# Products of 512 columns become two groups of 256 columns in the same bank

## The chip, the cores and the metric

The kernel runs on one core of a Trainium2 chip. The metric is device time in microseconds for one execution; lower is better. TensorE multiplies a stationary operand of 128 x 128, which a weight load brings in first, with a moving operand of up to 512 columns, and adds the result into one bank of PSUM (128 partitions, 512 float32 columns a bank). ScalarE (ACT) and VectorE (DVE) read PSUM, GpSimd (POOL) and SyncE (SP) start transfers.

## The reference

One block of a network on x of 4 x 2048 x 256 (float32):

```python
h = _layernorm(x, axis=-1) * (1 + ca) + sa
x = x + ga * _L0_attn_ref(h, ...)      # a gated linear recurrence over the 2048 steps
h = _layernorm(x, axis=-1) * (1 + cb) + sb
x = x + gb * _L0_ffn_ref(h, ...)       # 8 experts, each takes its best 512 rows of each of 4 batches
```

The recurrence: `u = h @ W_in`, two gates `sigmoid(u @ W_gx)` and `sigmoid(u @ W_ga)`, a scan over the steps, and `@ W_out`. The experts: softmax of scores over 8 experts, the 512 best rows of each expert and batch, `gelu(rows @ w1) @ w2` with a hidden width of 1024, weighted and added back into the rows.

## The kernel before, in words

It has two stages, written out engine by engine, with semaphores between the engines; the order on each engine is the order in the text.

The recurrence handles the 8192 rows in 16 groups of 512 (GT). In each of its steps TensorE transposes a group (line 1768), multiplies an earlier one by W_out (line 1852), forms two gates and u (`channels`, line 1749), and scores an older one (line 1874). `channels` computes two blocks (m) of 128 output channels; each block is one bank of PSUM and one call of `product`.

The experts are 32 units (8 experts x 4 batches), of 512 rows (CAPK) each. In unit u TensorE first transposes the gathered rows (line 1899), then does the second layer of the unit before (`layer2`, line 1925: 4 tiles of 128 rows, 24 matmuls of 256 columns each), then the first layer of its own (`layer1`, line 1953: 8 blocks m of 128 hidden channels, 6 matmuls of 512 columns each). Behind the first two blocks of most first layers stands `make_list` (line 428), 16 matmuls of 8 columns in bf16, for the unit after next. In the units at the start single bf16 matmuls (line 293) count hits for the choice of rows; they wait for VectorE.

Products are done in float32r with each operand split into a high and a low part: `PASSES` has the three pairs that are multiplied, so a product over 256 inputs (KD = 2 blocks) is 6 matmuls into one bank, the first with `start`, the last with `stop`. Behind the last one a semaphore tells ScalarE that the bank is full (`f_H` in the first layer); ScalarE takes the gelu (line 1210) and rounds it to the high part (line 1214), VectorE forms the low part (line 1540). Four banks are used in turn for the first layer (`h_bank`), and TensorE waits on `f_hf` before it fills one again.

Of the kernel before, what the change touches and what calls it, by code (L numbers as in the profile page):

```python
# [14 lines left out]
P = 128  # L15
# [33 lines left out]
def adaln_kernel(nc, x, W_in, b_in, W_gx, b_gx, W_ga, b_ga, a_param, W_out, b_out, gate_w, w1, w2, c, wmod, out):  # L49
# [5 lines left out]
    GT = 512  # L55
# [4 lines left out]
    CAPK = CAP * S // E  # L60
# [20 lines left out]
    with keep:  # L81
# [341 lines left out]
        def make_list(pe, u):  # L423

            for t in range(ST):
                if t % (ST // 2) == 0:
                    pe.wait_ge(f_pl, 2 * u + t // (ST // 2) + 1)
                ins = pe.matmul(list_psum(u), place[u % 2][:, t, :], vals_u[u % 2][:, t, :, :],  # L428
                                start=(t == 0), stop=(t == ST - 1))
            ins.then_inc(f_lm, 1)  # L430
# [33 lines left out]
        def sbr(name, shape, dt=F32):  # L464
            return recur.enter_context(nc.sbuf_tensor(name, shape, dt))
# [54 lines left out]
        hT_z = [sbr(f"hT_z{q}", [P, KD, GT], F32R) for q in range(2)]  # L520
# [89 lines left out]
        def rounds_in(s):  # L610

            n = [(s - PAIR_AT) * ROUNDS_IN - 2 + j for j in range(ROUNDS_IN)]
            return [v if 0 <= v < BITS else None for v in n]
# [10 lines left out]
        def sbf(name, shape, dt=F32):  # L624
            return moe.enter_context(nc.sbuf_tensor(name, shape, dt))

        w1_s = [[sbf(f"w1_0{q}", [P, KD, H], F32R) for q in range(2)]]
# [3 lines left out]
        xT = [sbf(f"xT{q}", [P, KD, CAPK], F32R) for q in range(2)]  # L631
# [86 lines left out]
        def h_bank(u, m):  # L718

            return H_bank[m % 4 if u else m % 2]  # L720
# [19 lines left out]
        def rounds_of(u):  # L740

            if u >= CHOSEN_IN:
                return [None] * 6
            here = [rounds_until(u) + j for j in range(PER_UNIT[u])]
            return here + [None] * (6 - len(here))
# [3 lines left out]
        with nc.Block() as block:  # L749
# [994 lines left out]
            def _(pe):  # L1744
                def product(out_, stationary, moving, first, last):

                    terms = [(k, q) for k in range(KD) for q in PASSES]
                    for j, (k, (qs, qm)) in enumerate(terms):
                        ins = pe.matmul(out_, stationary(qs, k), moving(qm, k), start=(first and j == 0),  # L1749
                                        stop=(last and j == len(terms) - 1))  # L1750
                    return ins

                def channels(out_, w, n=None, then=None):

                    for m in range(KD):
                        ins = product(out_[:, m, :], lambda q, k: w[q][:, k, m * P:(m + 1) * P], lambda q, k: hT_z[q][:, k, :],
                                      True, True)
                        if m == 0:
                            count(n)
                        if m == 0 and then is not None:  # L1760
                            then(pe, 0)
                    return ins
# [101 lines left out]
                def score(g):  # L1864

                    pe.wait_ge(r_x1T, g + 1)
                    pe.wait_ge(r_lo, min(g + 4, NG))
                    if g == 0:
                        pe.wait_ge(s_gw, 2)
                    if g >= 1:  # L1870
                        pe.wait_ge(r_sr, g)
                    for t in range(TT):
                        for k in range(KD):
                            ins = pe.matmul(S_tok[:, t, :], x1T[:, k, t * P:(t + 1) * P], Gb[:, g // GB, k, :],  # L1874
                                            start=(k == 0), stop=(k == KD - 1))
                    ins.then_inc(r_S, 1)

                def count(n):

                    if n is not None:  # L1880
                        sum_hits(pe, 0, n)
# [21 lines left out]
                def count_later(u, n):  # L1903

                    if n is not None:
                        pe.wait_ge(f_xf, u + 1)
                        sum_hits(pe, 1, n)
# [25 lines left out]
                def layer1(u):  # L1933

                    n = UNITS[u][0]
                    v = u + LISTED if u + LISTED < NU else None
                    late = u == CHOSEN_IN
                    pe.wait_ge(f_x, u + 1)
                    pe.wait_ge(f_ws, 4 * n + 2)
                    for m in range(KH):  # L1940
                        if u == 0 and m == 1:
                            score(NG - 1)
                        if v and m == (5 if u == 0 or late else 2):
                            make_list(pe, v)
                        if u == 0 and m >= 2:
                            pe.wait_ge(f_hf, m - 1)
                        elif u == 1 and m < 2:
                            pe.wait_ge(f_hf, KH + m - 1)
                        elif u >= 1:
                            pe.wait_ge(f_hf, KH * u + m + 1 - 4)  # L1950
                        terms = [(k, q) for k in range(KD) for q in PASSES]
                        for x_, (k, (qs, qm)) in enumerate(terms):
                            ins = pe.matmul(h_bank(u, m), w1_s[n % 2][qs][:, k, m * P:(m + 1) * P], xT[qm][:, k, :],  # L1953
                                            start=(x_ == 0), stop=(x_ == len(terms) - 1))
                        ins.then_inc(f_H, 1)
                        if u == 1 and m % 2 == 0:
                            count_later(u, rounds_of(u)[2 + m // 2])
                        if u != 1 and m in (1, 3, 5):
                            count_later(u, rounds_of(u)[3 + m // 2])
# [21 lines left out]
                for s in range(1, NG + 1):  # L1981
                    _, c_, _, d, e_ = stages(s)
                    n = rounds_in(s)
# [23 lines left out]
                    else:  # L2007
                        pe.wait_ge(r_p, c_)
                    channels(psA, Wa, n[0], sum_ties if s == NG else None).then_inc(r_A, 1)
                    if e_ is not None:  # L2010
                        pe.wait_ge(r_x1T, e_ + 1)
                    if c_ >= 1:
                        pe.wait_ge(r_tx, c_)
                    channels(psX, Wx, n[1], turn_probs if s == PAIR_AT else None).then_inc(r_X, 1)
                    if e_ is not None:
                        score(e_)
                    if s == NG:
                        sum_selected(pe, 0)
                    count(n[2])
                    pe.wait_ge(r_ta, c_ + 1)  # L2020
                    channels(psA, Wu, n[3], turn_slots if s == NG else None).then_inc(r_U, 1)
                    if s == 1:
                        mod_columns("ln2", 3)
# [15 lines left out]
                for u in range(NU):  # L2039
                    if u >= 1:  # L2040
                        turn(u)
                        layer2(u - 1, between_tiles(u))
                    layer1(u)
# [26 lines left out]
```

## Time and profile before

| | us |
|---|---|
| median of 3 runs | 1106.22 (1104.28 to 1106.46) |
| the profiled execution | 1105.63 |
| its span, first to last instruction | 1103.8 |
| TensorE busy in it | 1057.6 |
| mean granted clock of TensorE, as a share of full | 0.979 |

The span is cut into busy times of engines, a chain of waits followed back from the last instruction, and groups of instructions by line. A mean duration of a matmul is longer than its share of TensorE's time, since matmuls overlap; the spacing of a run of matmuls is its time divided by their number. In the chain a piece such as "PE psum L1925 x96" is a run of matmuls of one line in which nothing else was waited for.

### The profile page before, as it was taken

The page shows a single profiled execution, that of the slowest core. Times are in us where ns is not written, and L with a number is a line of the kernel's source. Part 1 is how long each engine was busy: PE and PEld are TensorE (multiplying, and loading weights), DVE is VectorE, ACT ScalarE, POOL GpSimd, SP SyncE. Part 2 cuts the span into 40 slices and gives each one's busy share as a digit, 9 for nine tenths or more (in the row PEclk, how much of TensorE's full clock was granted, in tenths as well). Part 3 has the DMA queues.
Part 4 walks back from the last instruction along what each step waited for, and adds up shares of the span by engine and source line. Part 5 has one row for each costly group of instructions (what it writes and reads, how often), then busy time and mean ns, then how long its engine had stood idle before and what let it go on. Part 6 is the DMA issues. An engine that isn't in the chain of part 4 may idle for free.

```text
span 1103.8 us, 18701 instructions
## 1 busy us (share of the span) xinstructions
PE 1057.6 (96%) x6922; PEld 932.2 (84%) x6922; DVE 726.5 (66%) x1680; ACT 781.1 (71%) x1237; POOL 461.2 (42%) x422
## 2 busy tenths in 40 slices
PE   7899999999798999999999999999999999999985
PEld 6778888888686888888999888999888999888875
DVE  5678999998767888965456455455455454477354
ACT  4658888887566777787666777775777766786741
POOL 2123432331343445444445444445544544454533
PEclk8999999999889999999999999999999999999988
DMA  7056756623348545555223545235343442379650
GB/s 253 10 124 191 232 146 141 154 59 57 78 124 102 149 116 121 157 123 125 55 40 80 123 87 138 53 81 136 80 111 80 92 102 39 69 216 309 160 186 39
DMA packets 96891, 130.85 MB, mean 119 GB/s; under 512 B 17312, under 2 KB 82464, under 8 KB 95776
## 3 DMA queue, kind: packets, MB, share of 16 engines
q1 hardware_dynamic: 62960, 84.11, 24.0%
q0 software_dynamic: 33024, 44.75, 23.2%
q8 instruction: 55, 0.90, 0.3%
q10 hardware_dynamic: 816, 0.79, 0.2%
q14 instruction: 36, 0.29, 0.1%
HBM read 78.96 MB, written 42.27 MB: 110 GB/s over the span
## 4 chain that ended last, share of the span: by engine, by line
PE 79%; DVE 7%; ACT 6%; issue 4%; DMA 2%; POOL 1%; SPq 1%; DVEq 0%; ACTq 0%; POOLq 0%
PE psum L1953 30%; PE psum L1925 30%; PE psum L1749 7%; PE psum L1852 4%; PE psum L1899 2%; PE psum L1768 2%; PE psum L1874 2%; DVE st L1237 1%; PE psum L428 1%; DMA w_raw<-ffn_rows 1%; DVE hs L1301 1%; DMA out_x<-res_t 1%; DVE x L1313 1%; ACT tx L1078 1%; ACT hT_z L1028 1%
## 5 line engine op out<-in xcount | busy, mean ns | idle before, releaser
L1925 PE MATMUL psum<-w,hidT 128*128 128x256 f32 x3072 | 374.1, 282 | 5.9 <-issue 4.5
L1953 PE MATMUL psum<-xT,w 128*128 128x512 f32 x1536 | 373.9, 399 | 4.9 <-DVE xT L1527 3.6
L1925 PEld LDWEIGHTS psum<-w,hidT 128*128 128x128 f32 x3072 | 364.9, 189 | 8.4 <-issue 6.4
L1953 PEld LDWEIGHTS psum<-xT,w 128*128 128x128 f32 x1536 | 286.5, 190 | 65.1 <-DVE xT L1527 3.8
L1540 DVE TENSOR_TENSOR hidT<-hf,hidT 128x512 fp32r<-128x512 f32 x256 | 176.5, 692 | 248.6 <-ACT hidT L1214 237.5
L960 POOL DMA_INDIRECT ffn_rows<-rows_y,idx_cur x120 | 210.7, 1755 | 229.4 <-issue 179.2
L450 POOL DMA_INDIRECT rows_in<-x_rows,idx_cur x128 | 139.4, 1089 | 177.5 <-DVE idx_cur L421 147.9
L1210 ACT ACTIVATE hf<-psum 128x512 f32<-128x512 f32 x256 | 151.2, 591 | 26.8 <-PE psum L1953 15.5
L1214 ACT ACTIVATE hidT<-hf 128x512 fp32r<-128x512 f32 x256 | 161.8, 632 | 8.1
L1116 ACT ACTIVATE rows_y<-psum,g_cur 128x256 f32<-128x256 f32 x124 | 51.9, 470 | 163.1 <-PE psum L1925 155.4
L410 DVE TENSOR_TENSOR place<-row_id,slot_u 128x1024 bf16<-128x1024 bf16 x64 | 76.3, 1222 | 1.1
L1484 DVE TENSOR_TENSOR w<-w_raw,w 128x1024 fp32r<-128x1024 f32 x60 | 71.4, 1220 | 0.3 <-issue 0.2
L1527 DVE TENSOR_TENSOR xT<-xf,xT 128x1024 fp32r<-128x1024 f32 x32 | 39.2, 1225 | 48.3 <-ACT xT L1106 46.6
L1145 ACT ACTIVATE w<-w_raw 128x1024 fp32r<-128x1024 f32 x60 | 60.1, 1046 | 12.3 <-DMA w_raw<-in_L_ffn_w 12.3
L1152 ACT ACTIVATE rows_in<-rows_in 128x256 f32<-128x256 f32 x128 | 66.3, 595 | 2.7 <-DMA rows_in<-x_rows,idx_cur 2.7
L1852 PE MATMUL psum<-Wout,hs 128*128 128x256 f32 x256 | 61.9, 398 | 2.4 <-ACT gb_bc L1091 2.4
L911 POOL TENSOR_SCALAR ve<-x 128x4 f32<-128x4 f32 x16 | 3.5, 222 | 139.6 <-DVE x L1241 139.5
L1055 ACT ACTIVATE ta<-psum,half_ba 128x512 f32<-128x512 f32 x32 | 20.3, 685 | 53.6 <-PE psum L1749 53.6
L1852 PEld LDWEIGHTS psum<-Wout,hs 128*128 128x128 f32 x256 | 50.2, 201 | 9.5 <-issue 2.6
L1749 PE MATMUL psum<-hT_z,Wa 128*128 128x512 f32 x192 | 52.4, 421 | 3.3 <-DVE p_t L1278 1.8
L1749 PE MATMUL psum<-hT_z,Wu 128*128 128x512 f32 x192 | 50.2, 405 | 0.0
L1100 ACT ACTIVATE xf<-psum,sbc,cb 128x512 f32<-128x512 f32 x64 | 45.9, 766 | 5.5 <-PE psum L1899 5.5
(206 smaller groups left out, 1225.3 us busy)
## 6 DMA issues: line engine op xcount, KB each, us to landing
w_raw<-in_L_ffn_w SPq DMA_DIRECT2D x30, 1024.0 KB, 11.3
x_rows<-x SPq DMA_DIRECT2D x16, 516.0 KB, 4.0
x_buf<-in_L_attn_x SPq DMA_DIRECT2D x16, 512.0 KB, 5.8
ffn_rows<-scratch SPq DMA_DIRECT2D x8, 1024.0 KB, 8.5
x_buf<-bias_bc POOLq DMA_DIRECT2D x16, 512.0 KB, 7.7
scratch<-x_rows SPq DMA_DIRECT2D x12, 512.0 KB, 8.6
out_x<-scratch SPq DMA_DIRECT2D x12, 512.0 KB, 7.9
w_raw<-ffn_rows SPq DMA_DIRECT2D x12, 512.0 KB
```

What stands on the lines that cost most here:

```text
L410: dve.tensor_tensor(place[n][:, at, :], row_id[:].unsqueeze(1).to_broadcast([P, ST // 2, P]), slot_u[n][:, at, :].to_broadcast([P, ST // 2 ...
L450: pool.indirect_dma_start(rows_in[u % 2][:, t, :], None, xr_dram[b], bass.IndirectOffsetOnAxis(ap=idx_cur[u % 4][:, t:t + 1], axis=0))\
L960: pool.indirect_dma_start(acc_dram[b], bass.IndirectOffsetOnAxis(ap=idx_cur[u % 4][:, t:t + 1], axis=0), rows_y[u % 2][:, t, :], None, com ...
L1152: ins = act.activation(x_u[:, t, 0:D], x_u[:, t, 0:D], ACT.Identity, bias=x_u[:, t, D:D + 1], scale=x_u[:, t, D + 1:D + 2])
L1210: act.activation(hf[m % HF][:], h_bank(u, m), ACT.Gelu_apprx_tanh).then_inc(f_hf, 1)
L1214: act.activation(hidT[0][:, m, :], hf[m % HF][:], ACT.Copy).then_inc(f_hh, 1)
L1484: dve.tensor_tensor(parts[1][:, at, :], raw[:, at, :], parts[0][:, at, :].bitcast(F32), ALU.subtract).then_inc(f_ws, 1)
L1540: dve.tensor_tensor(hidT[1][:, m, :], hf[m % HF][:], hidT[0][:, m, :].bitcast(F32), ALU.subtract).then_inc(f_hl, 1)
L1749: ins = pe.matmul(out_, stationary(qs, k), moving(qm, k), start=(first and j == 0), stop=(last and j == len(terms) - 1))
L1852: ins = pe.matmul(O_tok[:, t, :], hs[d % 2][:, k, t * P:(t + 1) * P], Wout[d // GB % 2][:, k, :], start=(k == 0), stop=(k == KD - 1))
L1925: ins = pe.matmul(y_tile(u, t), hidT[qs][:, k, t * P:(t + 1) * P], w2_s[n % 2][qm][:, k, :], start=(x_ == 0), stop=(x_ == len(terms) - 1))
L1953: ins = pe.matmul(h_bank(u, m), w1_s[n % 2][qs][:, k, m * P:(m + 1) * P], xT[qm][:, k, :], start=(x_ == 0), stop=(x_ == len(terms) - 1))
```

## The change

`channels` and `layer1` do each product in two halves of 256 columns: six matmuls for columns 0 to 255 of the bank, then six for columns 256 to 511. Each half has its own `start` and `stop`. The semaphore behind a first-layer product hangs on the last matmul of the second half, as the last of the product; in `channels` the count of hits comes behind both halves. The weights, the moving operand, the banks and the readers are as before.

```diff
                     for m in range(KD):
-                        ins = product(out_[:, m, :], lambda q, k: w[q][:, k, m * P:(m + 1) * P], lambda q, k: hT_z[q][:, k, :],
-                                      True, True)
+                        for half in (slice(0, GT // 2), slice(GT // 2, GT)):
+                            ins = product(out_[:, m, half], lambda q, k: w[q][:, k, m * P:(m + 1) * P],
+                                          lambda q, k: hT_z[q][:, k, half], True, True)
                         if m == 0:
                             count(n)
...
                         terms = [(k, q) for k in range(KD) for q in PASSES]
-                        for x_, (k, (qs, qm)) in enumerate(terms):
-                            ins = pe.matmul(h_bank(u, m), w1_s[n % 2][qs][:, k, m * P:(m + 1) * P], xT[qm][:, k, :],
-                                            start=(x_ == 0), stop=(x_ == len(terms) - 1))
+                        for half in (slice(0, CAPK // 2), slice(CAPK // 2, CAPK)):
+                            for x_, (k, (qs, qm)) in enumerate(terms):
+                                ins = pe.matmul(h_bank(u, m)[:, half], w1_s[n % 2][qs][:, k, m * P:(m + 1) * P], xT[qm][:, k, half],
+                                                start=(x_ == 0), stop=(x_ == len(terms) - 1))
                         ins.then_inc(f_H, 1)
```

## Rows read from the trace of the kernel before

**Rows 1.** The page's first part: busy us, share of the span, instructions.
```profile
PE 1057.6 (96%) x6922; PEld 932.2 (84%) x6922; DVE 726.5 (66%) x1680; ACT 781.1 (71%) x1237; POOL 461.2 (42%) x422
```
**Rows 2.** Busy time by stretch: two of the recurrence, then one unit.
```profile
core 0: us, PE busy (x) PEld busy (x) DVE busy (x) ACT busy (x) POOL busy (x), PEclk, DMA share, GB/s
93.00:108.40 15.40, 15.40 (x86) 13.34 (x85) 12.96 (x33) 12.33 (x18) 5.48 (x9) 1.00 0.56 155
187.50:203.60 16.10, 15.99 (x90) 13.20 (x89) 14.70 (x48) 13.55 (x21) 5.14 (x9) 1.00 0.44 127
643.20:666.94 23.74, 23.74 (x171) 21.49 (x170) 12.23 (x20) 17.33 (x30) 11.26 (x9) 1.00 0.40 90
```
**Rows 3.** Groups by line: count | busy us, mean ns of one | idle before.
```profile
L1925 PE MATMUL psum<-w,hidT 128*128 128x256 f32 x3072 | 374.1, 282 | 5.9 <-issue 4.5
L1953 PE MATMUL psum<-xT,w 128*128 128x512 f32 x1536 | 373.9, 399 | 4.9 <-DVE xT L1527 3.6
L1925 PEld LDWEIGHTS psum<-w,hidT 128*128 128x128 f32 x3072 | 364.9, 189 | 8.4 <-issue 6.4
L1540 DVE TENSOR_TENSOR hidT<-hf,hidT 128x512 fp32r<-128x512 f32 x256 | 176.5, 692 | 248.6 <-ACT hidT L1214 237.5
L1210 ACT ACTIVATE hf<-psum 128x512 f32<-128x512 f32 x256 | 151.2, 591 | 26.8 <-PE psum L1953 15.5
L1214 ACT ACTIVATE hidT<-hf 128x512 fp32r<-128x512 f32 x256 | 161.8, 632 | 8.1
```
**Rows 4.** The chain, 470 to 530 us: start us, us, what.
```profile
472.61 4.24 PE psum L1953 x18
...
477.73 10.89 PE psum L1925 x96
488.62 2.75 PE psum L1953 x12
491.37 0.40 PE psum L428 x16
491.77 8.36 PE psum L1953 x36
...
501.00 11.31 PE psum L1925 x96
512.31 2.80 PE psum L1953 x12
```
**Rows 5.** Groups by line, 483 to 487 and 506 to 510 us, TensorE.
```profile
L1925 PE MATMUL psum<-w,hidT 128*128 128x256 f32 x38 | 4.5, 276 | 0.0
...
L1925 PE MATMUL psum<-w,hidT 128*128 128x256 f32 x36 | 4.4, 281 | 0.0
```
**Rows 6.** The chain, 1016 to 1104 us.
```profile
1036.82 11.20 PE psum L1953 x48
...
1063.16 1.66 issue
```
**Rows 7.** The chain, 376 to 392 us.
```profile
378.27 0.88 PE psum L1899 x8
379.14 5.46 PE psum L1925 x48
384.60 0.02 PE psum L293
384.62 2.93 PE psum L1925 x24
```
**Rows 8.** The chain, 90 to 125 us.
```profile
93.47 5.57 PE psum L1749 x24
```
**Rows 9.** DMA queues: packets, MB, share of 16 engines.
```profile
q8 instruction: 55, 0.90, 0.3%
```
**Rows 10.** Waits over the span: us in total, times, longest.
```profile
PE psum L293 <- DVE hit L217: 5.5, 7, 1.1
```
**Rows 11.** Waits, 1040 to 1104 us.
```profile
PEld psum L1925 <- issue: 5.9, 9, 1.2
```

## The prediction

> **What bounds the kernel now.** I read the shares of busy time first: TensorE is busy 96% of the span and no other engine more than 71% [rows 1]. A share is a mean over stages, so I looked at single stages. In each stretch read of the first half (the recurrence) TensorE is busy without a gap or nearly so, and in the experts a whole unit of 23.74 us has 23.74 us of TensorE, at the full clock (1.00, 2.4 GHz), while ScalarE and VectorE have 6 and 11 us to spare [rows 2]. A microsecond added to the stream of products is therefore a microsecond of the kernel, and one taken away is a gain. The chain of waits agrees: its pieces in the experts are nothing but TensorE's lines [rows 4].
>
> So the question is one of spacing: how long from one product's start to the next. The groups by line say that 3,072 products of 256 columns (second layer) keep TensorE busy as long as 1,536 of 512 columns (first layer): 374.1 and 373.9 us [rows 3]. Column for column the two sizes cost the same; the mean durations (282 and 399 ns) overlap and must not be multiplied. These totals hide two different spacings, which the chain shows piece by piece [rows 4]:
> - 256 columns: 96 products in 10.89 us (113.4 ns each) in one unit and in 11.31 us (117.8 ns each) in the next, with nothing waited for in either. I call these the short and the long spacing. Mean durations change with them, 276 and 281 ns [rows 5].
> - 512 columns: 12 products that follow without a break take 2.75 us (229.2 ns) behind short ones and 2.80 us (233.3 ns) behind long ones. Where the list's 16 small products stand before them, they go back to the short spacing: pieces of 18 and 36 take 4.24 and 8.36 us, so 18 more cost 4.12 us, 228.9 ns each, with 0.12 us for the restart. A piece of 48 with no list in it stays long throughout (11.20 us, 233.3 ns) [rows 6].
>
> The spacing is thus a state that lasts until something breaks the stream, and that is newly chosen behind each break. I can't derive from the trace what chooses it.
>
> **The change, part by part.** It removes 1,536 + 576 products of 512 columns and adds twice as many of 256: 2,112 more products and as many more weight loads. Nothing else is issued: waits, signals, banks and readers stay, since the signal hangs on the last product of the second half and the count of hits stands behind both halves. No DMA and no queue is moved.
>
> *Weight loads.* They double in both places. The second layer already has a load for each 256 columns, and its loads (364.9 us busy) lie under 374.1 us of products [rows 3]; their cost is inside 113.4 or 117.8 ns, so I add nothing. If that cover failed, it would already show in the second layer.
>
> *First layer, 32 units of 8 products of 6.* Doubled, the short spacing gives 226.8 ns where one wide product takes 228.9, and the long one 235.6 where it takes 233.3. The sign hangs on the state. In a unit of the steady half, the first 12 become 24 that follow the second layer unbroken: 24 x 117.8 = 2.83 us against 2.80 if that is long (+0.03). The other 36 become 72 behind the list's break: 0.12 + 72 x 117.8 = 8.60 us if long (+0.24), 0.12 + 72 x 113.4 = 8.28 us if short (-0.08). I take long: the nearest row of 256 columns behind a small bf16 product is the pair of pieces behind the count of hits, 24 in 2.93 us, which less the same 0.12 us is 117 ns each; the piece before them, behind a transpose, is 48 in 5.46 us (113.8 ns) [rows 7]. Units before the steady half have most of their wide products short too, so 32 x 0.27 = 8.6 us; a product there sometimes waits for VectorE's count of hits (5.5 us over 7 waits [rows 10]), which hides a little, so +8.
>
> *Second layer.* Untouched, 0, if its state stays in each unit. What precedes it does change, and that is the largest unknown: a unit that goes from long to short gains 11.31 - 10.89 = 0.42 us, over some 24 units -10 us; the few short ones going long cost at most 2.
>
> *Recurrence, 576 products.* 24 take 5.57 us [rows 8], 232.1 ns each. Two narrow ones: 226.8 to 235.6, so from -3.1 to +2.0 us. Its breaks are again small products and counts, which stand nearest to [rows 7], so I take the long end; some of it hides in the stage's few waits: +1.
>
> *Evacuation.* A first-layer product of six takes 1.39 us (8.36 / 6); ScalarE's two passes over it take 0.591 + 0.632 = 1.22 us and VectorE's one 0.692 [rows 3]. Both stay under the new 1.36 to 1.41 us, so neither becomes the bound.
>
> *Supply of instructions.* 4,224 more instructions come through the queue that has 55 packets and 0.90 MB now [rows 9]; I take 0, since the second layer runs at that density for 11 us on end. Beside it stands the one stretch near the end where TensorE stops in small pieces with no releaser shown: pieces of "issue" up to 1.66 us [rows 6], and idle of 5.9 us in that window [rows 11]. If lack of instructions is its cause, it may grow or move: from -8 to +15 us.
>
> Sum: 8 + 0 + 1 = +9 us on the profiled execution's 1105.6 us (span 1103.8 and 1.8 around it): 1114.6. The median of the runs shown lies 0.6 us higher than that execution, well inside the other errors, so I leave the number.
>
> The rows show the extra as a state; the Trainium skill has a constant instead. Its page "TensorE: Matmul & The Clock Gate", section "Wait — 56ns, not 53.3ns?", puts a fixed cost of about 2.5 ns on every matmul at the full clock, whatever its columns. That speaks against splitting: 2,112 x 2.5 = 5.3 us, an estimate from that page, and 1110.9 us. The long rows agree with it (2 x 117.8 - 233.3 = 2.3 ns), the short ones (2 x 113.4 - 228.9 = -2.1 ns) do not.
>
> **The rivals.**
> - *The second layer's restart falls into the short spacing.* For: the pieces behind the transposes before the steady half are short: three of 48 in 5.46 us, of which one stands in [rows 7], and the 96 in 10.89 us of [rows 4]. Against: from 501 us on every steady unit is long. Per steady unit: second layer -0.42, the first 24 at 113.4 (2.72 against 2.80) -0.08, the other 72 long +0.24: -0.26; 24 units -6.2, the other eight +1.6, the recurrence +1 to -3: -4 to -8, 1098 to 1102 us. This ends on the other side. It decides as soon as more than about half of the steady units turn.
> - *The first layer goes short behind the list, the second stays long*, as wide products do there now. Per unit +0.03 - 0.08 = -0.05, over 32 units -1.6, recurrence +1 to -3: 1101 to 1105 us.
> - *Both go short.* 24 x -0.58 = -13.9, the rest -1 to -4: about 1089 us.
> - *Instructions run short* in the denser stream: the stretch near the end comes twice, or longer: +9 with 8 to 15 more, 1123 to 1130 us. Against it: no unnamed idle in the second layer elsewhere.
>
> **How the numbers follow.** Forecast (long behind the list, second layer as it is) 0.42; second layer turns short 0.26; only the first layer short 0.14; both short 0.11; instructions 0.07. The predicted time is the forecast's, 1114.6, with its own range 1109 to 1119 from the bounds of the recurrence and of the early units. For 8 in 10 I take in the second and third case and leave out the last two: 1096 to 1119. Faster by over 0.2% (2.2 us, about what a measurement of this kernel can tell from no change): 0.24 of the second case, 0.06 of the third, 0.11 of the fourth, 0.41. Within 0.2%: 0.02 and 0.08, 0.10. Slower: 0.42 and 0.07, 0.49.
>
> **What would show it.** In the profile after, the steady units' chain should have 24 products of line 1953's successor in about 2.83 us, 72 in 8.60 us, and 96 of the second layer still in 11.31 us; a unit of 24.0 us. Mean durations of 281 ns in both layers mean long, 276 short. If 72 take 8.28 us or the second layer 10.89 us, the state was misjudged, not the bound. Wrong altogether would be a unit in which TensorE has gaps, or a spacing of 256 columns outside 113 to 118 ns.

## The result, and the profile after

The changed kernel takes 1096.08 us (median of 4 runs, 1095.47 to 1098.32) where the kernel before takes 1106.34 beside it: a ratio of 0.9917, 95% interval [0.9904, 0.993]. It is 10 us faster where 8 us slower was forecast. The time lies outside the forecast's own range (1109 to 1119) and just inside the lower edge of the wider one (1096 to 1119), on the side that the forecast did not take.

The page of the profiled execution (span 1094.4 us; before 1103.8) begins with busy us, share and instructions of each engine, which answers to [rows 1]:

```profile
PE 1049.2 (96%) x9034; PEld 1030.4 (94%) x9034; DVE 726.0 (66%) x1680; ACT 779.2 (71%) x1237; POOL 462.4 (42%) x422
```

TensorE has 2,112 more products and still bounds. What it was given is seen only by stretch. This account is made from the starts of the same products in both traces:

| stretch | before to after, us |
|---|---|
| start to the first layer of unit 0 (recurrence) | -0.35 |
| to the first layer of unit 8 | +1.2 |
| units 8 to 27 | -5.6 |
| units 28 and 29 | +1.3 |
| first layer of unit 30 to the last second layer | -7.8 |
| last second layer and the end | +1.8 |

The chain after, 640 to 690 us (start us, us, what), answers to [rows 4]. L1926 is the second layer, L1955 the first, with the list left out, L1900 the transposes:

```profile
642.96 10.90 PE psum L1926 x96
653.86 2.72 PE psum L1955 x24
...
656.98 8.27 PE psum L1955 x72
665.25 0.87 PE psum L1900 x8
666.12 11.31 PE psum L1926 x96
677.43 2.83 PE psum L1955 x24
...
680.66 8.59 PE psum L1955 x72
```

The first unit is short in all three pieces (10.90, 2.72, 8.27), the second long in all three (11.31, 2.83, 8.59). The state lives through the list and is chosen anew behind the transposes. The units come as short, short, long, over and over: 23.16, 23.17 and 24.00 us, a mean of 23.44, where every steady unit before took 23.74.

The chain of the recurrence, to set beside [rows 8]:

```profile
93.33 5.70 PE psum L1749 x48
...
100.71 2.95 PE psum L1749 x24
```

The piece that took 5.57 us takes 5.70, so 118.8 ns a product: a third value, outside the 113 to 118 of the experts.

The chain after, near the end, to set beside the stops of [rows 6]:

```profile
1033.38 10.89 PE psum L1955 x96
...
1045.14 2.40 PE psum L1926 x21
1047.54 2.14 issue
1049.68 8.79 PE psum L1926 x75
1058.47 8.79 PE psum L1955 x72
```

The many small stops are gone. One of 2.14 us is left, at the 21st product, and the other 75 run through. The second layer of unit 30 takes 13.3 us from its first product to its last, before 19.2. Of the 7.8 us of this stretch it holds 5.9; the first layer of unit 31, after it, holds 1.4.

A part of both is TensorE's clock. The chain before has these two pieces behind the stops:

```profile
1065.55 2.71 PE psum L1925 x11
1068.26 12.30 PE psum L1953 x48
```

And by stretch (two of before, then the second layer of unit 30 after: us, TensorE busy and its products, granted clock, DMA share, GB/s):

```profile
1059.30:1064.10 4.80, 1.99 (x11) 1.00 0.62 209
1064.20:1070.90 6.70, 5.95 (x20) 0.50 0.46 177
1044.90:1058.30 13.40, 11.26 (x99) 1.00 0.48 180
```

Before, TensorE was idle for more than half of 4.8 us, and then the granted clock stood at 0.50 (1.2 GHz) from 1064.1 to 1071.0 us. There 11 products take 2.71 us where the long spacing gives 1.30, and the first layer of unit 31 takes 12.30 us where a piece of 48 takes 11.20 [rows 6]. So some 2.5 us of the 7.8 (1.4 + 1.1, an estimate from these pieces) are the lower clock behind the stops and not the stops themselves. The changed kernel runs this work at 1.00; it has a fall of 3.4 us earlier, from 1015.2 us, in the stretch of units 28 and 29 that came out 1.3 us longer.

### The profile page after: what moved, and what is told of

Same layout as the page of the kernel before. It is cut to its first block, busy times and chain, and to the rows that moved or that the text cites. A ratio compares the mean times of both kernels' runs of the same rounds, so it can differ in the third digit from the quotient of the medians.

```text
span 1094.4 us, 22925 instructions
## 1 busy us (share of the span) xinstructions
PE 1049.2 (96%) x9034; PEld 1030.4 (94%) x9034; DVE 726.0 (66%) x1680; ACT 779.2 (71%) x1237; POOL 462.4 (42%) x422
## 4 chain that ended last, share of the span: by engine, by line
PE 82%; DVE 5%; ACT 5%; issue 3%; DMA 2%; POOL 1%; SPq 0%; DVEq 0%; ACTq 0%; POOLq 0%
PE psum L1955 30%; PE psum L1926 29%; PE psum L1749 10%; PE psum L1853 4%; PE psum L1875 2%; PE psum L1900 2%; PE psum L1769 2%; PE psum L428 1%; DMA w_raw<-ffn_rows 1%; DVE st L1237 1%; ACT hf L1210 1%; PE psum L1803 1%; DMA out_x<-res_t 1%; ACT rows_in L1152 1%; DVE x L1313 0%
## 5 line engine op out<-in xcount | busy, mean ns | idle before, releaser
L1955 PE MATMUL psum<-xT,w 128*128 128x256 f32 x3072 | 374.5, 281 | 6.3 <-DVE xT L1527 3.6
L1955 PEld LDWEIGHTS psum<-xT,w 128*128 128x128 f32 x3072 | 363.8, 190 | 6.9 <-DVE xT L1527 3.8
L1926 PE MATMUL psum<-w,hidT 128*128 128x256 f32 x3072 | 365.4, 280 | 4.2 <-issue 2.1
L1926 PEld LDWEIGHTS psum<-w,hidT 128*128 128x128 f32 x3072 | 357.7, 188 | 5.1 <-DVE hidT L1540 2.8
L960 POOL DMA_INDIRECT ffn_rows<-rows_y,idx_cur x120 | 212.9, 1774 | 225.8 <-issue 177.4
L450 POOL DMA_INDIRECT rows_in<-x_rows,idx_cur x128 | 136.9, 1069 | 177.2 <-DVE idx_cur L421 147.5
L1853 PE MATMUL psum<-Wout,hs 128*128 128x256 f32 x256 | 59.5, 386 | 2.4 <-ACT gb_bc L1091 2.4
L1749 PE MATMUL psum<-hT_z,Wa 128*128 128x256 f32 x384 | 54.1, 298 | 4.2 <-DVE Wu L1340 2.0
L1749 PEld LDWEIGHTS psum<-hT_z,Wa 128*128 128x128 f32 x384 | 50.5, 197 | 5.7 <-DVE hT_z L1267 2.9
L1749 PE MATMUL psum<-hT_z,Wu 128*128 128x256 f32 x384 | 50.6, 286 | 0.0
```

The costliest lines, as they stand in the source:

```text
L450: pool.indirect_dma_start(rows_in[u % 2][:, t, :], None, xr_dram[b], bass.IndirectOffsetOnAxis(ap=idx_cur[u % 4][:, t:t + 1], axis=0))\
L960: pool.indirect_dma_start(acc_dram[b], bass.IndirectOffsetOnAxis(ap=idx_cur[u % 4][:, t:t + 1], axis=0), rows_y[u % 2][:, t, :], None, com ...
L1853: ins = pe.matmul(O_tok[:, t, :], hs[d % 2][:, k, t * P:(t + 1) * P], Wout[d // GB % 2][:, k, :], start=(k == 0), stop=(k == KD - 1))
L1926: ins = pe.matmul(y_tile(u, t), hidT[qs][:, k, t * P:(t + 1) * P], w2_s[n % 2][qm][:, k, :], start=(x_ == 0), stop=(x_ == len(terms) - 1))
L1955: ins = pe.matmul(h_bank(u, m)[:, half], w1_s[n % 2][qs][:, k, m * P:(m + 1) * P], xT[qm][:, k, half], start=(x_ == 0), stop=(x_ == len(te ...
```

## The experiments

Each run has its own measurement of the kernel before on the same chip. All ratios are to that, with the 95% interval. Patterns and times within a kernel come from the one profiled execution of each run; the mean unit runs from the second layer of unit 7 to that of unit 27. "Unit 30" is the time from the first to the last product of its second layer; "gathers" is how long behind that first product GpSimd starts the gathers of unit 31.

| run | ratio | steady second layers | mean unit, us | unit 30, us | gathers, us |
|---|---|---|---|---|---|
| before | 1 | all long | 23.74 | 19.2 | 5.3 |
| after | 0.9917 [0.9904, 0.993] | short, short, long | 23.46 | 13.3 | 10.4 |
| e14 (after again) | 0.9922 [0.9901, 0.9944] | short, short, long | 23.46 | 12.5 | 8.8 |
| e1 | 0.9894 [0.9878, 0.9909] | short, short, long | 23.46 | 12.7 | 8.8 |
| e2 | 0.9996 [0.9984, 1.0008] | all long | 23.74 | 18.2 | 5.3 |
| e3 | 0.9905 [0.9885, 0.9925] | all short | 23.50 | 12.9 | 9.5 |
| e4 | 1.0003 [0.9992, 1.0014] | all long | 23.77 | 18.5 | 5.3 |
| e5 | 0.9963 [0.9949, 0.9977] | short, short, long | 23.46 | 19.4 | 5.3 |
| e6 | 0.9942 [0.9926, 0.9959] | all long | 23.74 | 13.3 | 10.4 |
| e7 | 0.9913 [0.9897, 0.993] | all short | 23.53 | 12.8 | 9.9 |
| e8 | 0.9973 [0.9953, 0.9993] | long, short | 23.81 | 12.7 | 8.9 |
| e10 | 0.988 [0.986, 0.99] | all short | 23.25 | 12.9 | 9.4 |
| e11 | 0.9884 [0.9864, 0.9904] | all short | 23.27 | 13.2 | 10.1 |
| e12 | 0.9943 [0.9923, 0.9963] | long but the first | 23.72 | 12.7 | 9.5 |
| e15 | 0.9953 [0.9936, 0.9969] | short, short, long | 23.46 | 19.6 | 5.3 |
| e16 | 0.9999 [0.999, 1.0009] | all long | 23.74 | 21.6 | 5.3 |
| e17 | 0.992 [0.9903, 0.9936] | long but the first | 23.72 | 10.9 | 5.3 |
| e18 | 0.9939 [0.9921, 0.9957] | long but the first | 23.72 | 14.6 | 10.0 |
| e20 | 0.9978 [0.9961, 0.9995] | long but the first | 23.72 | 11.6 | 12.7 |
| e21 | 1.0008 [0.9995, 1.002] | all long | 23.74 | 19.3 | 5.3 |

### What chooses the state

Theory A: the state is chosen at each break of the stream, and hangs on the timing of that break, so a delay of some 25 ns changes the pattern. Theory B: the width of the products fixes it. (Theory C in the texts below, that the gain lies in the stops near the end, is taken up behind this part.)

**Each part of the change alone.** e1 leaves `channels` as before, e2 leaves `layer1` as before.

```diff
-                        for half in (slice(0, GT // 2), slice(GT // 2, GT)):
-                            ins = product(out_[:, m, half], lambda q, k: w[q][:, k, m * P:(m + 1) * P],
-                                          lambda q, k: hT_z[q][:, k, half], True, True)
+                        ins = product(out_[:, m, :], lambda q, k: w[q][:, k, m * P:(m + 1) * P], lambda q, k: hT_z[q][:, k, :],
+                                      True, True)
```

> Only the first layer's products are halved; gates and u stay 512 columns wide. Theory A (each break of the stream picks the short or the long spacing anew by its timing, and the width has no say in it): the recurrence gets back the 0.18 us per step that the halves cost there (two pieces of 5.57 and 2.90 us against 5.70 and 2.95), some 2 to 3 us over 16 steps, and the experts show some mixture of short and long units again, not necessarily the one of the changed kernel: 1089 to 1104 us. Theory B (narrow products in the first layer bring the second layer into the short spacing): two units in three short as in the changed kernel, 1093 to 1095 us. Theory C (the gain lies in the stretch near the end, where the kernel before stops 8 us with no releaser): 1100 us or less only if that stretch is free of stops here too.

```diff
-                        for half in (slice(0, CAPK // 2), slice(CAPK // 2, CAPK)):
-                            for x_, (k, (qs, qm)) in enumerate(terms):
-                                ins = pe.matmul(h_bank(u, m)[:, half], w1_s[n % 2][qs][:, k, m * P:(m + 1) * P], xT[qm][:, k, half],
-                                                start=(x_ == 0), stop=(x_ == len(terms) - 1))
+                        for x_, (k, (qs, qm)) in enumerate(terms):
+                            ins = pe.matmul(h_bank(u, m), w1_s[n % 2][qs][:, k, m * P:(m + 1) * P], xT[qm][:, k, :],
+                                            start=(x_ == 0), stop=(x_ == len(terms) - 1))
```

> Only gates and u are halved; the first layer stays 512 columns wide. Theory B: the experts are as in the kernel before, all steady units long in the second layer, 23.74 us each, and the recurrence costs 2 to 3 us more: 1108 to 1110 us. Theory A: the same recurrence, but the experts begin at another moment, so the steady units may go short in the second layer, 23.3 us each instead of 23.74: anything from 1097 to 1110 us. Theory C: if the stops near the end come from where TensorE stands in its stream of instructions, they may go away here, -6 to -8 us, with the units as before.

e1 has the whole gain, its pattern and the missing stops; e2 is at 0.9996, so halving gates and u alone changes nothing that can be measured. (The changed kernel's two ratios, 0.9917 and 0.9922, stand 2.5 to 3 us above that of e1; their intervals overlap with its own, and whether the gates' halves cost that much beside the others is open.) All that follows is in the first layer.

**A break 25 ns longer.** The list's first matmul is issued twice, in the changed kernel (e3) and in the one before (e4).

```diff
+                for _ in range(1 if t == 0 else 0):
+                    pe.matmul(list_psum(u), place[u % 2][:, t, :], vals_u[u % 2][:, t, :, :], start=True, stop=True)
                 ins = pe.matmul(list_psum(u), place[u % 2][:, t, :], vals_u[u % 2][:, t, :, :],
```

> The changed kernel with the first of the list's 16 small matmuls issued twice, so that each list's break lasts about 25 ns longer (32 lists, 0.8 us in all; the first of the two is overwritten). Theory A: the pattern of units (short, short, long) changes, all short (23.2 us each, 1091 us) or all long (24.0 us each, 1102 to 1106 us) or another mixture. Theory B: the pattern stays and the time is 1097 us.

> The kernel before with the same extra small matmul in each list, and no product halved. Theory A: the steady units, all long before, may turn short in the second layer (10.89 instead of 11.31 us), wholly or in part: 1096 to 1107 us, and then without any change of width. Theory B: all stay long, 1107 us. Theory C: the stops near the end change, since 64 instructions more lie before them: up to 8 us less with the units as before.

The chain of e3 (L1928 is the second layer, L1957 the first, L429 the extra matmul):

```profile
644.45 10.90 PE psum L1928 x96
655.34 2.72 PE psum L1957 x24
658.06 0.02 PE psum L429
...
658.49 8.59 PE psum L1957 x72
```

One small matmul more and the repeating three units are gone: every steady second layer is short, every piece of 72 long, so here the state changes at the list, which it did not do in the kernel without the extra matmul. That goes with theory A. The kernel with wide products does not move with the same edit, though: in e4 the second layers stay long, and the 36 products behind the list take 8.36 us as before. So what stands in the break matters, but the same addition does not act alike on both streams. An extra matmul adds an instruction and some 25 ns at once; no run tells the two apart.

**Two and three more**, with the gates wide (`range(2 ...)` and `range(3 ...)` in the same place, on e1).

> The first layer halved and gates wide, and each list's first small matmul issued three times, so each list's break is 50 ns longer (1.6 us over 32 lists). If the spacing behind a break is chosen by its timing, the pattern of units (short, short, long without the extra) changes: all short gives 23.2 us a unit and 15 us faster than before, all long 24.0 us and no gain. If the timing has no say, 9 to 10 us faster, with the same pattern.

> The same with the first small matmul issued four times, 75 ns longer a break (2.4 us in all). Chosen by timing: again another pattern, between 23.2 and 24.0 us a unit, from 14 us faster to no gain. Not chosen by timing: 8 to 9 us faster with the pattern short, short, long.

Two give the pattern of e3 (mean unit 23.53 us), three a new one: long, short, long, short (24.07 and 23.55 us). Breaks that differ by one small matmul a step thus gave three patterns, with the same products and the same columns. It is not the chance of one execution: the five traces with halves in the steady units and the breaks as they were (after, e14, e1, e5, e15) all have short, short, long.

**A break of another kind, ahead of the transposes.** One (e10) or two (e11) matmuls of 8 columns, whose result is overwritten, on e1.

```diff
+                    for _ in range(1 if u >= 2 else 0):
+                        pe.matmul(turned_in(u)[:, 0, 0:8], same_e[:], before_e[:, 0:8], start=True, stop=True)
                     for t in range(CT):
                         for k in range(KD):
                             ins = pe.transpose(turned_in(u)[:, k, t * P:(t + 1) * P], rows_in[u % 2][:, t, k * P:(k + 1) * P],
```

> First layer halved, gates wide, and one more small bf16 matmul (8 columns, constants, its result overwritten) ahead of the transposes of each unit from 2 on: the break before the second layer is 25 to 40 ns longer, the list's break is as it was. If the spacing is chosen by the break's timing, the units' pattern changes. Wanted: all units short, 23.2 us each where two in three are now, 5 us less than without the extra, some 16 us faster than the kernel before. Also possible: all long, no gain over before but the 6 us near the end.

> The same with two such matmuls, 25 ns more. If chosen by timing: another pattern again, 23.2 to 24.1 us a unit, 16 to 5 us faster than the kernel before. If the timing has no say: short, short, long as without the extra, 10 us faster.

e14 is the changed kernel once more, on their chip.

> The changed kernel itself on the same chip as the others, to see whether halving gates and u costs: the recurrence's pieces are 0.18 us a step longer than with wide gates, 0 to 3 us over 16 steps. 8 to 11 us faster than the kernel before.

The chain of e10 (L1927 second layer, L1956 first, L1898 the extra matmul):

```profile
661.52 0.02 PE psum L1898
661.55 0.93 PE psum L1901 x8
662.47 10.91 PE psum L1927 x96
673.38 2.72 PE psum L1956 x24
...
676.50 8.27 PE psum L1956 x72
```

All steady units are short in all pieces. The extra matmul and the longer transposes cost 0.08 us a unit (0.02 + 0.93 against 0.87), and the mean unit still falls from 23.46 to 23.25. e10 is the fastest kernel of the study by its median, 1089.28 us on a chip where the changed kernel takes 1094.59 and the kernel before 1103.51; its interval overlaps with those of e1 and e11. That one small matmul in a break changes the state behind it is shown (e10 against e1, e3 against after). What selects the state remains open, and it is not what stands in the break alone: in the changed kernel the same break gives short twice and long once, and the second layer of unit 7 is long in before, e6, e16 and e21 and short in e12, e17, e18 and e20, though TensorE's instructions up to there are the same in all eight.

### Where the other gain is: the stops near the end

**Halves in part of the units** (gates wide). The condition after `if` is `u < 29` in e5, `u >= 29` in e6, `u == 30` in e12, `u != 30` in e15, `u in (29, 31)` in e16, `u == 30 and m >= 4` in e18.

```diff
-                        for half in (slice(0, CAPK // 2), slice(CAPK // 2, CAPK)):
+                        for half in ((slice(0, CAPK // 2), slice(CAPK // 2, CAPK)) if u < 29 else (slice(0, CAPK),)):
```

> The first layer's products are halved in units 0 to 28 only; units 29 to 31 and the gates stay 512 columns wide. It splits the gain in two: the spacing in the steady units, and the stretch near the end where the wide kernels lose 6 to 8 us in TensorE's second layer of unit 30 with no releaser shown. If the stretch hangs on when TensorE gets there (5 to 6 us earlier here), it is free of stops: 10 to 11 us faster than the kernel before. If it hangs on the width of the products of these units themselves, the stops stay: 4 to 6 us faster only.

> The reverse: halved in units 29 to 31 only. The steady units are as in the kernel before, 23.74 us each, so TensorE reaches the end when it does there. If the stretch hangs on the width of its own products, the stops go: 5 to 7 us faster than before. If it hangs on when TensorE gets there, they stay: within 1 us of before.

> Halved in unit 30 alone (the one whose first layer ends where the stretch of stops begins); all else 512 columns wide. If the stops hang on the products right before them, they go: 6 us faster than the kernel before. If they hang on those of unit 29 or 31 or on all three, they stay in part or whole: 0 to 3 us faster.

> First layer halved in every unit but unit 30, gates and u wide. With the halves in unit 30 alone the stops of TensorE in that unit's second layer were gone (12.74 us for 96 products, against some 19). If unit 30's own first layer decides, whatever the other units do, the stops return here: second layer of unit 30 in 18 to 20 us, and a ratio of about 0.9894 + 6 / 1104 = 0.995. If it was a stray of timing or of the place in the stream of instructions, they may stay away: 12 to 13.5 us, and 0.989.

> The kernel before with the first layer halved in units 29 and 31 alone, 96 more products of 256 columns in place of 48 each. If unit 30's own first layer decides, the stops stay: second layer of unit 30 in 18 to 20 us, ratio 0.999 to 1.001. If any denser first layer near the end takes them away: 12 to 13.5 us, ratio about 0.994.

e5 and e6 split the gain: 3.5 us for 29 units of patterns, 6.6 us for the last three units (1105.44 less 1101.9 and 1098.81). e12 has 1103.51 less 1096.9, 6.6 us, from 48 products becoming 96 in unit 30 alone. e15 and e16 are the other side: with unit 30 wide the stops are there, whatever its neighbours do. The chain of e15, second layer of unit 30:

```profile
1042.67 4.55 PE psum L1925 x40
...
1054.21 0.81 issue
1055.02 1.10 PE psum L1925 x4
...
1057.48 1.10 issue
```

**As many instructions, but wide products** (e17, on the kernel before), and **half of the halves** (e18, above).

```diff
+                        for _ in range(6 if u == 30 else 0):
+                            pe.matmul(h_bank(u, m)[:, 0:8], same_e[:], before_e[:, 0:8], start=True, stop=True)
                         for x_, (k, (qs, qm)) in enumerate(terms):
```

> The kernel before with six small bf16 matmuls of 8 columns ahead of each of the eight products of unit 30's first layer (they write the bank that the product then starts anew): as many instructions as with the halves, but wide products. The list's 16 small ones take 0.40 us, so 48 take 1.2 us more. If the number of instructions in that unit decides, the stops go: second layer in 12 to 13.5 us, -6.6 + 1.2 us, ratio 0.995. If the halves themselves (two short groups in place of one) decide, the stops stay: 18 to 20 us, ratio 1.000 to 1.002.

> The kernel before with the last four of the eight products of unit 30's first layer halved, the first four wide: half of the edit that took the stops away. If it is a matter of amount, about half of the 6.6 us: second layer of unit 30 in 15 to 17 us, ratio 0.997. If what stands right ahead of the second layer decides, all of it: 12 to 13.5 us, ratio 0.994. If the first four decide, none: 18 to 20 us, ratio 1.000.

The chain of e17: the small matmuls cost their 0.15 us for each six, and the second layer runs through.

```profile
1048.56 0.15 PE psum L1953 x6
1048.70 1.50 PE psum L1955 x6
...
1051.08 10.90 PE psum L1925 x96
```

So it is not the halves as such: 48 small matmuls in that first layer, which does the same products as before, take the stops away too, and so do 24 more products in its second half. It is no matter of amount either: e18 has the gain of e12 (0.9939 and 0.9943). Its layer takes 14.6 us because of one wait of 1.79 us at the 21st product and a granted clock of 0.50 for 3.4 us behind it.

**Who stands beside the stops.** GpSimd's part of the timeline before (start us, us, line, operation, in square brackets the idle time ahead of it) has this in the stretch of the stops. L973 and L976 are the gathers of sums and rows:

```profile
1053.96 1.08 POOL L973 DMA_INDIRECT place<-ffn_rows,idx_cur  x1 [1.59 <-issue]
...
1059.11 0.94 POOL L976 DMA_INDIRECT rows_in<-x_rows,idx_cur  x1 [0.30 <-issue]
1060.36 0.95 POOL L976 DMA_INDIRECT rows_in<-x_rows,idx_cur  x1 [0.30 <-issue]
...
1062.87 0.94 POOL L976 DMA_INDIRECT rows_in<-x_rows,idx_cur  x1 [0.30 <-issue]
```

And the chain before has its long stops in nearly the same rhythm, some 1.3 us (the next one is the 1.66 us of [rows 6]):

```profile
1059.37 0.42 issue
1059.79 0.72 PE psum L1925 x4
1060.51 0.70 issue
1061.21 0.72 PE psum L1925 x4
1061.94 0.75 issue
```

In the timeline after, the first gather of unit 31 comes 10.4 us behind the layer's start, not 5.3:

```profile
1055.29 1.07 POOL L973 DMA_INDIRECT place<-ffn_rows,idx_cur  x1 [6.00 <-issue]
```

Two runs move one thing each behind the second layer of unit 30, in the kernel before: e20 these gathers, e21 the last four stores to the output, which also start inside the stops.

```diff
+                    if u == NU - 1:
+                        pool.wait_ge(f_Y, 2 * NU - 2)
                     pool.wait_ge(f_lm, NU)
```

> The kernel before with one wait more on GpSimd: the eight indirect gathers of unit 31 (sums and rows) start when the second layer of unit 30 is through. In the trace of before they start 5.3 us behind that layer's first product and are issued every 1.25 us, and the stops of TensorE come at 10.4, 11.6, 13.0 and 14.2 us, in the same rhythm; in the kernels without stops they mostly start 9 to 10 us behind it. If the gathers hold TensorE up, the stops go: second layer 11 to 13.5 us in place of 19, ratio 0.994 to 0.996 (the end may wait for the later gathers). If they only stand beside it: 18 to 20 us, ratio 1.000 or above. In the one kernel with small matmuls in unit 30 they start 5.3 us behind the first product too and nothing stops, which speaks for the second.

```diff
                 for k in range(GB, NG):
+                    if k == NG - GB:
+                        sp.wait_ge(f_Y, 2 * NU - 2)
                     store(k)
```

> The kernel before with one wait more on SP: the last four stores of 512 KB to the output start when the second layer of unit 30 is through, where the first of them starts at 1055.5 us in the trace of before, inside the stops. If these stores, or they and the gathers together, hold TensorE up: second layer 11 to 13.5 us, ratio about 0.994. If not: 18 to 20 us, ratio 1.000 to 1.003.

The chain of e20 (L1927 is the second layer, L1955 the first):

```profile
1046.56 4.55 PE psum L1927 x40
1051.11 0.50 issue
1051.61 6.54 PE psum L1927 x56
...
1069.55 2.88 another core or an unknown queue
...
1073.11 0.78 another core or an unknown queue
```

Without the gathers beside it the layer takes 11.6 us in place of 19.2, with wide products. Without the stores nothing changes (19.3). The gathers are needed for the stops; that is shown, though not whether it is GpSimd's work on them or the transfers that they start. e20 gains only 0.9978, because they now run beside unit 31's first layer, where ACT's values come late (the pieces of 2.88 and 0.78 us) and TensorE waits in turn, from 1068.9 to 1075.95.

**How a first layer of 96 moves them.** This path is read from the traces alone. Before gathering, GpSimd waits for `f_g`: the copy of line 1535, which VectorE does behind unit 30's last hidden block and behind unit 31's transposed rows. VectorE's part of the last hidden block, and the copy, after:

```profile
1048.93 0.69 DVE L1540 TENSOR_TENSOR hidT<-hf,hidT 128x512 fp32r<-128x512 f32 x1 [2.96 <-issue]
...
1054.26 0.16 DVE L1535 COPY g_cur<-rows_in 128x4 f32<-128x4 f32 x1
```

And before:

```profile
1049.35 0.69 DVE L1540 TENSOR_TENSOR hidT<-hf,hidT 128x512 fp32r<-128x512 f32 x1 [0.70 <-issue]
...
1052.93 0.16 DVE L1535 COPY g_cur<-rows_in 128x4 f32<-128x4 f32 x1
```

ACT's steps ahead of them (its last gelu of the unit, and the first step on unit 31's transposed rows), two rows of after and then two of before:

```profile
1047.64 0.60 ACT L1210 ACTIVATE hf<-psum 128x512 f32<-128x512 f32 x1 [2.40 <-remote]
1050.54 1.45 ACT L1100 ACTIVATE xf<-psum,sbc,cb 128x512 f32<-128x512 f32 x2 [1.64 <-remote]
1048.06 0.60 ACT L1210 ACTIVATE hf<-psum 128x512 f32<-128x512 f32 x1
1049.22 1.43 ACT L1100 ACTIVATE xf<-psum,sbc,cb 128x512 f32<-128x512 f32 x2
```

Counted from the first product of the second layer (1048.65 us before, 1044.90 after), VectorE starts the last block 0.7 us behind it before and 4.0 after, with 0.70 and 2.96 us of idle time ahead of it, and the copy comes 4.3 and 9.4 us behind. What holds it is ACT, which stands for 2.40 and 1.64 us after and not at all before; "remote" says that the trace shows no releaser, and the product that the gelu reads was done at 1044.27 us. TensorE's stop of 2.14 us at the 21st product is the other end of the same hold: the program lets the second layer's 22nd product wait for VectorE's last block, which ends at 1049.62 us, and TensorE goes on at 1049.68. So a small hold of ACT puts the gathers off by 5.1 us, until the second layer is nearly done. In all eleven runs with more than 48 products in unit 30's first layer TensorE waits at the 21st product, the gathers start 8.8 to 10.4 us behind the layer's start, and the stops beside them are gone; in all seven with 48 wide ones and the gathers and stores where they were, or the stores alone moved, they start at 5.3 and the stops are there. e17 is the exception to this path: its gathers start at 5.3 us and nothing stops. Its second layer was through 10.9 us behind its start, about where the long stops of the others begin (8 to 11 us), but why it was not slowed in the first half I can't say. Open, too, is what holds ACT for some 2 us behind a first layer of more products, and how a gather holds up a product.

## Why the prediction was wrong

- **The bound** was right: TensorE is 96% busy before and after, and in the steady units each microsecond of its stream is one of the span.
- **The prices** were right. The four given for the pieces were 2.72 and 2.83, 8.28 and 8.60 us; the trace has 2.72, 2.83, 8.27 and 8.59, and 10.90 or 11.31 in the second layer. Doubling the weight loads cost nothing: 96 products of the halved first layer take 10.89 us (unit 30, above), as 96 of the second layer did before [rows 4].
- **The choice of the state** is the step that failed in the steady units. "I take long", from the nearest broken piece [rows 7], and "0, if its state stays" for the second layer, were both a guess at what the text itself said it couldn't derive. Two units in three went short in all pieces. The second layer then gives -0.41 in two units of three, so -0.27 a unit; the first layer -0.17 in two and +0.26 in one, so -0.03. That is -0.30 a unit in place of +0.27, 20 x -0.30 = -6 us; the account has -5.6. The first rival named the right part (the second layer's restart) and had a chance of 0.26; it took all units short there and long behind the list, which is what e3 does, not the changed kernel.
- **The stretch near the end** is the larger miss. The text named it, bounded it at -8 to +15 us and took 0; it came out 7.8 us shorter. It also held that no DMA is moved: none is added, but the gathers of unit 31 start 5.1 us later in the layer. Its suspected cause, a lack of instructions, is not what the runs point to: more instructions made the stops go away (e17), moving the gathers did so too (e20), and the traces of e15 and e16 have no packet of the instruction queue in the stretch of the long stops. It left out as well that the granted clock falls to 0.50 behind the stops, some 2.5 us by the estimate above. The prediction looked at TensorE's row alone and did not lay GpSimd's issues beside the stops, though their rhythm of 1.25 us stood in the trace of before.
- **The recurrence** was put at +1, with bounds of -3.1 to +2.0. The one piece rose by 0.13 us, and the stage came out 0.35 us shorter; alone it can't be told from no change (e2). That 256 columns would stay within 113 to 118 ns was wrong there: 118.8.
- **Evacuation** did not bind, as said: ACT stays at 71% and VectorE at 66%.

The Trainium skill, page "TensorE: Matmul & The Clock Gate", section "Wait — 56ns, not 53.3ns?", would have the split cost about 2.5 ns a matmul, which the prediction put at +5.3 us. The long pieces of this trace agree with it and the short ones do not: 2 x 117.8 - 233.3 = 2.3 ns and 2 x 113.4 - 228.9 = -2.1 ns. Which of the two a unit falls into outweighs the rule: 0.84 us a unit between short (23.16) and long (24.00).

The forecast's sum and its gap: +8 for the first layer came out near -1 with the second layer's -5 in the steady units, and the 0 for the end came out as -7.8. The other stretches of the account give 4 us of that back.

## What to carry to other kernels

Where a product has two lasting spacings, the price of an edit is the state that each stretch falls into, and no row before tells it; forecast both, and try one tiny matmul at a break, which here took another 0.2 us off each unit (e10 against e1). Where the bounding engine stops without a releaser, lay the issues of every other engine and the granted clock beside the stops before choosing a term of 0. An edit in one unit can move the transfers of the next, so look at the time at which a gather starts, not only at its own length.

## What the runs showed of the hardware

- 256-column products of float32r held one of two spacings, 113.4 or 117.8 ns, for a whole piece of 96, at a granted clock of 1.00 [rows 2]; the choice changed with one matmul of 8 columns (25 ns) in the break (e1 against e10), and not in the kernel with wide products (e4). In the recurrence the spacing was a third one, 118.8 ns.
- Eight indirect gathers, issued every 1.25 us, stood beside a second layer that took 18 to 22 us, with stops of up to 1.7 us that show no releaser; with them put off, the same 96 products took 11.6 us (e20). In e17 they stood beside a layer of 10.9 us without a stop. In the waits of the kernel before, ACT was held in that stretch as well, once for 7.7 us, by nothing that the trace shows.
- Behind those stops, with TensorE busy for 1.99 of 4.8 us, the granted clock of the kernel before fell to 0.50 (1.2 GHz) for 6.8 us. In the trace of e2 the stops came without the fall, and unit 30's second layer to unit 31's took 29.3 us in place of 31.8.
- The fastest kernel of the study by its median, with halves in the first layer alone and one 8-column matmul ahead of the transposes, is at 0.988 [0.986, 0.99] of the kernel before.
